# Routed tokens: from a placement table with gathered rows to a DRAM region per expert with dense tiles

## What is computed

```
logits = flat @ gate_W.T                       # 8 experts
probs = softmax(logits);  top_v, top_i = top_k(probs, 2)
g = silu(flat @ w1_e[e]);  u = flat @ w3_e[e]  # F = 512
out_e = (g * u) @ w2_e[e]
routed = sum over the two chosen experts of top_v * out_e
shared = the same form with shared weights, 512 wide in all, / 8
ffn = 0.5 * shared + 0.5 * routed
```

## Time and profile before

| | us |
|---|---|
| median of three timed runs | 782.5 (780.04 to 783.66) |
| the profiled execution, span from first to last instruction | 859.9 |
| TensorE busy | 717.7 (83%) |
| VectorE busy | 447.1 (52%) |
| ScalarE busy | 348.5 (41%) |
| GpSimd busy | 427.7 (50%) |

### The profile page before, as it was taken

How to read it: one execution, slowest core, us unless ns; L and a number is a source line. 1 busy time by engine, 2 the same in 40 slices (tenths; PEclk the granted TensorE clock), 3 DMA queues, 4 the chain that set the end, 5 groups by cost and what they waited for, 6 DMA issues and landing times.

```text
span 859.9 us, 12865 instructions
## 1 busy us (share of the span) xinstructions
PE 717.7 (83%) x4282; PEld 591.9 (69%) x4282; DVE 447.1 (52%) x1089; ACT 348.5 (41%) x913; POOL 427.7 (50%) x499
## 2 busy tenths in 40 slices
PE   3863998988888988985887687998998988888996
PEld 3742877877776767873565475786876777777874
DVE  7689743323233333425999977953333332323437
ACT  3622622323333233445775535831333332323433
POOL 6439052465555646347898524033365656555430
PEclk9985898999999999997999997998999999999999
DMA  9600010111111111021110010001111111111128
GB/s 317 230 1 0 1 37 17 30 43 37 40 38 37 42 34 44 25 85 58 40 39 24 26 50 0 2 25 25 28 41 35 43 34 43 37 40 36 31 71 247
DMA packets 45021, 43.75 MB, mean 51 GB/s; under 512 B 5984, under 2 KB 39776, under 8 KB 44576
## 3 DMA queue, kind: packets, MB, share of 16 engines
q1 hardware_dynamic: 35872, 24.32, 9.2%
q0 software_dynamic: 9088, 18.63, 7.8%
HBM read 27.33 MB, written 15.60 MB: 50 GB/s over the span
## 4 chain that ended last, share of the span: by engine, by line
issue 40%; PE 36%; DVE 8%; ACT 3%; another core or an unknown queue 2%; DMA 1%; SPq 0%; POOL 0%; DVEq 0%; ACTq 0%
PE psY L1463 8%; PE psH L1446 4%; PE psH L1375 3%; PE psG L1306 3%; PE psG L1304 2%; PE psG L1305 2%; PE psU L1306 2%; PE psU L1304 2%; PE psU L1305 2%; DVE rec L1045 1%; PE psG L1529 1%; PE psU L1562 1%; ACT silu L1190 1%; PE psT L1403 1%
## 5 line engine op out<-in xcount | busy, mean ns | idle before, releaser
L638 POOL DMA_INDIRECT results<-yout,target x142 | 139.7, 984 | 182.3 <-DVE yout L949 144.2
L745 DVE TENSOR_TENSOR hr<-silu,psU 128x512 f32<-128x512 f32 x142 | 97.3, 685 | 252.2 <-ACT silu L1190 129.4
L623 POOL DMA_INDIRECT rows<-tokens,source x142 | 137.0, 965 | 137.8 <-issue 69.0
L1463 PE MATMUL psY<-W,hT 128*128 x1120 | 152.6, 279 | 18.2 <-issue 12.2
L1190 ACT ACTIVATE silu<-psG 128x512 f32<-128x512 f32 x142 | 85.1, 599 | 203.6 <-PE psG L1306 148.7
L1463 PEld LDWEIGHTS psY<-W,hT 128*128 128x128 f32 x1120 | 135.9, 192 | 29.6 <-issue 22.9
L1183 ACT ACTIVATE hT<-psH 128x512 f32<-128x512 f32 x142 | 84.7, 596 | 110.5 <-remote 57.2
L1446 PE MATMUL psH<-ident,hr 128*128 128x128 f32 x568 | 86.4, 275 | 26.4 <-DVE hr L745 26.4
L1446 PEld LDWEIGHTS psH<-ident,hr 128*128 128x128 f32 x568 | 68.6, 141 | 53.2 <-DVE hr L745 37.8
L745 DVE TENSOR_TENSOR hs<-silu,psU 128x512 f32<-128x512 f32 x64 | 43.4, 683 | 59.0 <-PE psU L1306 30.8
L1375 PEld LDWEIGHTS psH<-W2S,hs 128*128 128x128 f32 x512 | 65.9, 210 | 8.1 <-DVE hs L745 6.9
(11 more groups left out here) (187 smaller groups left out, 1266.1 us busy)
## 6 DMA issues: line engine op xcount, KB each, us to landing
W<-w_e SPq DMA_DIRECT2D x3, 2048.0 KB, 13.4
tokens<-XN SPq DMA_DIRECT2D x16, 256.0 KB, 3.1
Y<-results SPq DMA_DIRECT2D x32, 128.0 KB, 2.3
YF<-results SPq DMA_DIRECT2D x16, 256.0 KB, 5.1
rows<-tokens,source POOLq DMA_INDIRECT x142
results<-yout,target POOLq DMA_INDIRECT x142
X<-x SPq DMA_DIRECT2D x8, 256.0 KB, 5.6
out<-X SPq DMA_DIRECT2D x8, 256.0 KB, 2.6
```

Of the source, the lines that this page charges most:

```text
L623: pool.indirect_dma_start(rows[:, g % RING, t, :], None, tokens, bass.IndirectOffsetOnAxis(ap=source[:, tile:tile + 1], axis=0))\
L638: pool.indirect_dma_start(results, bass.IndirectOffsetOnAxis(ap=target[:, tile:tile + 1], axis=0), yout[:, g % 2, t, :], None).then_inc(y_ ...
L745: dve.tensor_tensor(hidden, silu[:, s.u % 2, :], psU[:, s.u % 2, :], ALU.mult).then_inc(h_done, 1)
L1463: i = pe.matmul(into[:, t * D:(t + 1) * D], hT[:, s.u % 2, f, :], W2[:, bass.ds(at + f * D, D)], start=(f == 0), stop=(f == FT - 1))
```

## The change

A token row gets two more words, its own number and its second place (ROW = 130). DRAM holds a region of 4224 rows for each expert (`slots`). Routing is done in five batches of 4, 4, 8, 8 and 8 token tiles (`ROUTES`): for each, VectorE finds the top two and, after TensorE's count, the place of each pair in its expert's region, and GpSimd scatters each token tile twice, once for each chosen expert, with one indirect DMA each (`scatter`, 64 a layer). The tiles of an expert are then dense rows of its region, whose start VectorE works out once (`find_tiles`, 20 operations). SyncE writes 128 rows of zeros at the end of each expert's rows and fetches each tile with a plain DMA from an address that it loads from SBUF (`fetch_rows`). The targets of the results are found group by group from the two words that come with the rows (`aim_group`, four small operations on VectorE). The placement table, its batches on three engines, the tensor `tokens` and its eight writes a layer are gone. The low parts of the transposed tokens are made by VectorE and not by GpSimd; of the expert weights ScalarE makes the high parts and VectorE the low parts. GpSimd keeps the scale factors of the layer norm and sends the results, with no fetches between. The gate product has 8 columns and not 128. Steps are placed by the tables below, from a few steps before the first shared step. `FRONT` and the rest of the routed part stay as they were.

```diff
+ROUTES = [(0, 4), (4, 4), (8, 8), (16, 8), (24, 8)]
+WIDEST = max(n for _, n in ROUTES)
+ROW = D + 2
+REGION = NT + P
+SLOTS = E * REGION
...
+FIRST = [-5, -7]
+LN_AT = [{-5: 0, -4: 1, -3: 2, -1: 3, 2: 4, 5: 5, 8: 6, 12: 7, 14: 8}, {-6: 7, -3: 8}]
+TOP_AT = [{-2: 0, 1: 1, 7: 2, 13: 3, 20: 4}, {-7: 0, -2: 1, 2: 2, 7: 3, 13: 4}]
+PLACE_AT = [{0: 0, 3: 1, 9: 2, 15: 3, 22: 4}, {-4: 0, 1: 1, 4: 2, 9: 3, 15: 4}]
+LOW_AT = [{-1: 0, 1: 1, 4: 2, 8: 3, 11: 4, 16: 5, 19: 6, 25: 7}, {-5: 0, -1: 1, 0: 2, 2: 3, 6: 4, 10: 5, 14: 6, 18: 7}]
+LOW_W_AT = {5: 0, 7: 1, 9: 2, 10: 3, 13: 4, 16: 5, 17: 6, 20: 7}
+TABLES_AT = [24, 17]
+GATES_AT = [26, 19]
+TURN_AT = [{-4: 0, -3: 1, 0: 2, 5: 3, 8: 4, 12: 5, 15: 6, 18: 7}, {-5: 6, -3: 7}]
+SCORE_AT = [{-3: 0, -2: 1, 2: 2, 6: 3, 9: 4, 13: 5, 18: 6, 20: 7}, {-6: 5, -2: 6, 0: 7}]
+RANK_AT = [{-1: 0, 3: 1, 10: 2, 16: 3, 23: 4}, {-5: 0, 2: 1, 6: 2, 11: 3, 17: 4}]
+HIGH_AT = [SCORE_AT[0], {-6: 0, -5: 1, -3: 2, -2: 3, 2: 4, 6: 5, 10: 6, 14: 7}]
+HIGH_W_AT = {k - 2: j for k, j in LOW_W_AT.items()}
+EXP_AT = [25, 18]
...
+                def fetch_rows(g):
+                    if g >= RING:
+                        sp.wait_ge(aimed, GROUPS * l + g - RING + 1)
+                    for tile in range(g * GT, min((g + 1) * GT, RUN)):
+                        at = sp.value_load(from_row[0:1, tile:tile + 1], min_val=0, max_val=SLOTS - P)
+                        sp.dma_start(rows[:, g % RING, tile % GT, :], slots[bass.ds(at, P), :])\
+                          .then_inc(rows_in[g % RING], 16)
+                sp.wait_ge(ends_done, l + 1)
+                for e in range(E):
+                    end = sp.value_load(ends[0:1, e:e + 1], min_val=0, max_val=SLOTS - P)
+                    sp.dma_start(slots[bass.ds(end, P), :], zeros[:, :]).then_inc(padded, 16)
+                sp.wait_ge(padded, 16 * E * (l + 1))
+                sp.wait_ge(from_done, l + 1)
+                sp.wait_ge(scattered, 16 * TOPK * TILES * (l + 1))
+                sp.wait_ge(u_full, shared_at(l, (RING + 1) * FT - 1) + 1)
+                for g in range(GROUPS):
+                    fetch_rows(g)
...
+                def scatter(b, first, last):
+                    start, n = ROUTES[b]
+                    if first == 0:
+                        pool.wait_ge(xn_done, CHUNKS * l + (start + n) // CH)
+                        pool.wait_ge(placed, len(ROUTES) * l + b + 1)
+                    for tile in range(start + first, start + last):
+                        for k in range(TOPK):
+                            pool.indirect_dma_start(
+                                slots, bass.IndirectOffsetOnAxis(ap=place[:, tile, 2 * k:2 * k + 1], axis=0),
+                                XN[:, tile, :], None).then_inc(scattered, 16)
+                def scale_next(c):
+                    if l == 0 or c >= POOL_AHEAD:
                         scale_ln(l, Step.of(c, 2))
+                for c in range(3):
+                    scale_next(c)
                 if l == 0:
...
+                    low_shared()
+                scale_next(3)
+                if l == 1:
+                    for c in range(4, CHUNKS):
+                        scale_next(c)
+                    for b, (_, n) in enumerate(ROUTES):
+                        scatter(b, 0, n)
+                else:
+                    scatter(0, 0, 4)
+                    scale_next(4)
+                    scatter(1, 0, 2)
+                    scale_next(5)
+                    scatter(1, 2, 4)
+                    scatter(2, 0, 2)
+                    scale_next(6)
+                    scatter(2, 2, 4)
+                    scale_next(7)
+                    scatter(2, 4, 8)
+                    scatter(3, 0, 8)
+                    scatter(4, 0, 8)
...
+                    if t == 0:
+                        pool.wait_ge(aimed, GROUPS * l + g + 1)
...
+                for g in range(GROUPS):
+                    for t in range(min(GT, RUN - g * GT)):
+                        send_result(g, t)
...
+                def top_two(b):
...
+                    if b > 0:
+                        dve.wait_ge(ranked, len(ROUTES) * l + b)
+                    route.then(dve.tensor_reduce(counted[:, :], both, X_AXIS, ALU.add))
+                    dve.tensor_copy(chosen_rows[:, :], counted[:, :]).then_inc(picked, 1)
...
+                def place_in(b):
+                    start, n = ROUTES[b]
...
+                    from_ = region[:, :] if b == 0 else taken_to[:, b - 1, :]
+                    dve.wait_ge(ranked, len(ROUTES) * l + b + 1)
+                    route.then(dve.tensor_tensor(base[:, :], from_, psY[:, RANKS_AT:RANKS_AT + E], ALU.add))
+                    dve.tensor_tensor(taken_to[:, b, :], from_, psY[:, RANKS_AT + E:RANKS_AT + 2 * E], ALU.add)\
+                       .then_inc(ranks_read, 1)
+                    route.then(dve.tensor_tensor(both[:, :, 0], base[:, :], both[:, :, 0], ALU.add))
+                    route.then(dve.tensor_tensor_scan(sums, not_first[n][:, :, :].rearrange("p e i -> p (e i)"),
+                                                      chosen[:, 0:n * E], 0.0, ALU.mult, ALU.add))
+                    for k in range(TOPK):
+                        route.then(dve.tensor_tensor(picks, sums.rearrange("p (e i) -> p i e", e=E),
+                                                     onehot[k][:, at, :], ALU.mult))
+                        route.then(dve.tensor_reduce(posf[:, at, k], picks, X_AXIS, ALU.add))
+                    route.then(dve.tensor_copy(place[:, at, 0:3:2], posf[:, at, :]))
+                    dve.tensor_copy(XN[:, at, D:ROW].bitcast(i32), place[:, at, 1:3]).then_inc(placed, 1)
...
+                def aim_group(g):
+                    tiles = slice(g * GT, min((g + 1) * GT, RUN))
+                    n = tiles.stop - tiles.start
+                    dve.wait_ge(rows_in[g % RING], fetched(l, g))
+                    if g == 0:
+                        dve.wait_ge(tables_done, l + 1)
+                    aims.then(dve.tensor_tensor(aim[:, 0, 0:n], rows[:, g % RING, 0:n, D + 1].bitcast(i32), own[:, tiles],
+                                                ALU.is_equal))
+                    aims.then(dve.scalar_tensor_tensor(aim[:, 1, 0:n], aim[:, 0, 0:n], float(NT),
+                                                       rows[:, g % RING, 0:n, D].bitcast(i32), ALU.mult, ALU.add))
+                    aims.then(dve.tensor_tensor(aim[:, 2, 0:n], aim[:, 1, 0:n], valid[:, tiles], ALU.mult))
+                    dve.tensor_tensor(target[:, tiles], aim[:, 2, 0:n], dump[:, tiles], ALU.add).then_inc(aimed, 1)
...
+                for k in range(FIRST[l], SHARED):
                     if k == front[l] + 6 % FT:
                         copy_xT(Step.of(0, 2 * GT))
+                        aim_group(0)
+                    if k in PLACE_AT[l]:
+                        place_in(PLACE_AT[l][k])
                     if k == done[0]:
                         shared_steps(1)
-                    for _ in range(PLAN[l].get(k, 0)):
-                        batch(taken)
-                        taken += 1
-                    if k == TABLE_STEP[l]:
-                        table()
-                        experts()
+                    if k in TOP_AT[l]:
+                        top_two(TOP_AT[l][k])
+                    if k in LN_AT[l]:
+                        ln_step(LN_AT[l][k])
+                    if k in LOW_AT[l]:
+                        low_xnT(LOW_AT[l][k])
+                    if l == 0 and k in LOW_W_AT:
+                        low_experts(LOW_W_AT[k])
+                    if k == TABLES_AT[l]:
+                        find_tiles()
+                    if k == GATES_AT[l]:
+                        weigh()
...
+                def high_experts(j):
+                    w, cols = j % 2, slice(j // 2 * WCOLS, (j // 2 + 1) * WCOLS)
+                    act.wait_ge(experts_in, 48)
+                    act.activation(W13H[:, w, cols], W13[:, w, cols], ACT.Copy).then_inc(w_high, 1)
```

More of the change, by code:

```diff
@@ L317, in macaron @@
              ("ha", [P, 2, TB * P], fp32)],
-            [("rows", [P, RING, GT, D], fp32)],
+            [("rows", [P, RING, GT, ROW], fp32)],
             [("XNTL", [P, NT], fp32r), ("XNTH", [P, NT], fp32r)])
@@ new lines, in find_tiles @@
+                def find_tiles():
+                    cmp3 = [P, TILES_R, E]
+                    last = taken_to[:, len(ROUTES) - 1, :]
+                    dve.wait_ge(ranks_read, len(ROUTES) * (l + 1))
+                    dve.tensor_scalar(ends[:, :], last, 1.0, None, ALU.add).then_inc(ends_done, 1)
+                    route.then(dve.tensor_tensor(counted[:, :], last, region[:, :], ALU.subtract))
+                    route.then(dve.tensor_scalar(tile_bits[:, 0, :], counted[:, :], float(P - 1), None, ALU.add))
@@ L929, in copy_xT_later, with aim_later @@
                         copy_xT(s)
+                def aim_later(s):
+                    if s.i > 0 and s.u % GT == 0:
+                        aim_group(s.over(GT))
```

(60 more changed lines are left out.)

437 lines of the change are left out of this document (142 added, 295 removed).

## The result

| | before | after |
|---|---|---|
| timed runs, median us | 782.09 (4 runs, 780.04 to 783.66) | 817.35 (4 runs, 814.8 to 818.64) |
| ratio to before | | 1.0444 [1.0424, 1.0465] |
| profiled execution, us | | 818.64 |
| span, granted clock | | 816.9 us, 0.942 |

The forecast was 798, slower; the range ended at 814. The direction and the main mechanism held; the size did not: of a loss of 35 us some 16 were expected.

A forecast was written before the change was run, and what follows sets the result against it. Placement masks on VectorE bound layer 0's front, TensorE the routed stage. Timed: 782.5 - 5.1 (layer 0) + 20.4 (layer 1) = 797.8 us, taken as 798; likeliest 790 to 812, wider range 752 to 814.

The forecast's parts named there:

- first step: Stalls of 66.1 + 7.6 + 6.4 = 80.1 us explain the profile's extra 77.4 us and are absent from timed runs.
- Rival 1: Indirect DMAs cost less without the profiler: 768 at 1.0 us each, some 766 at 0.8; chance 0.20.
- rival 3: Scatters cost 1.5 us, by the wider row or by locking: total 823 us; chance 0.10.
- layer 0, from there to the last scatter's end: Layer 0's front: 48 scatters x 1.27 = 61 us plus three ln scale factors, 3.1 us.
- layer 0, tail to the first routed product: Layer 0, behind the last scatter: landings, four SyncE loads and issues, transposes and splitting, sum 11.4 us.
- layer 1, chain: Layer 1's front: 64 scatters on GpSimd's queue, 63 x 1.27 + 0.97 = 81 us.
- 588.0 - 508.0: Layer 1 before the change: first routed product without the stall at 588.0, last attention addition ending at 508.01.
- With 4 us of waiting for X and the first scores: 51.: Layer 0's front: VectorE needs 43 us from 3.9 to place routes 0 to 2, plus 4 us of waits.
- So GpSimd is never without work.: Layer 1's front: route 4, placed some 44 us after the first, meets a queue of 48 scatters (61 us).
- Four transposes and two splitting operations ... 2.0.: Last part of the wait behind the last scatter, before the first routed product: 0.6 + 2 x 0.69 = 2.0 us.
- The rule weighed against the change: 2-port VectorE operations lock GpSimd out: 20 scalings lengthen layer 0's chain by up to 7.4 us, sum 805.
- only for this reason the removed masks bring so little: Layer 0's front: VectorE's 96 us of work ends about 105, covered by scatters whose last comes at 115.

The follow-up runs named there:

- experiment 1: The kernel before, unchanged, profiled a second time: 780.09 us, span 778.1.
- 3: The changed kernel with each of the 16 scatters of the fifth batch issued twice in each layer, the second into an unread spare tensor: 856.71 us.
- 8: The changed kernel with only the first of the two scatters of each token tile in layer 1, 32 instead of 64: 794.25 us.
- 2: The changed kernel with the last output block of each shared front moved ahead of the first transposes: 813.91 us.
- 4: The changed kernel with 28 instead of 24 shared steps ahead of layer 1's routed stage: 816.83 us.
- 6: The changed kernel with layer 1's second and third token batch placed one and two steps earlier: 811.84 us.
- 7: The changed kernel with VectorE's 8 weight-split subtractions replaced by a one-input operation that writes zeros: 814.01 us.
- 5: The kernel before with only the expert-weight splits moved off GpSimd, to 8 casts on ScalarE and 8 subtractions on VectorE: 759.95 us.

## Why the prediction was right in direction and wrong in size

**Right.** Its first step, that the 77 us by which the profile was long do not belong to the timed runs, is shown by experiment 1. So is the mechanism: 64 scatters a layer, 1.26 us apart, set both first routed products (3 and 8). The price per scatter, taken from the nearest row of another kind of indirect DMA, was right to 0.01 us, with rows of 520 bytes. Rival 1 (cheaper) and rival 3 (1.5 us) fall with it. The routed stages came out as said.

**Wrong: what stands around the 64 x 1.27.** Sizes, from the prediction's terms:

| term | predicted | measured | more |
|---|---|---|---|
| layer 0, start of the third batch | 51 | 56.8 | 5.8 |
| layer 0, from there to the last scatter's end | 64 | 66.1 | 2.1 |
| layer 0, tail to the first routed product | 11.4 | 14.0 | 2.6 |
| layer 1, last addition to first scatter | 8.0 | 9.5 | 1.5 |
| layer 1, chain | 81 | 87.5 | 6.5 |
| layer 1, tail | 11.4 | 13.9 | 2.5 |

Together 21.0. The 56.8 is the latest of six profiles with the same code up to there; the others (2, 3, 4, 6 and 8) have 55.4 to 56.5, so about 1 us of the first row is the difference between executions. Against before, in this profile layer 0 lost 5.0 instead of gaining 5.1 and layer 1 lost 32.2 instead of 20.4 (before itself stands 1.3 better there than the 588.0 - 508.0 assumed); the stretch between and the end add 1.7. The steps that failed:

- "With 4 us of waiting for X and the first scores: 51." A sum of busy times with a guess for the waits. VectorE's waits up to 57 us in after are 4.5 us for shared products, 4.3 for a GpSimd constant, 2.9 for the first scores and 1.4 for X: 13.1, where 3.9 and 4 were counted. This is 5.2 of the 5.8 in this profile.
- "So GpSimd is never without work." It was asked of route 4 only, the last. Batches 1 and 2 came too late by 1.8 and 4.4 us more than the usual 0.30; placing them one and two steps earlier took 5.5 us off the total (6).
- "Four transposes and two splitting operations ... 2.0." What the transposes stand ahead of was not followed: an output block of 32 products was queued behind their wait, 5.4 to 5.6 us long instead of 3.8, since TensorE had stood for over 20 us (granted clock 0.62 in 120:140). SyncE's part came out lower: 5.3 us from the first issue (125.60) to the transposes (130.85), where 8.1 had been put down, though that first issue came 2.7 us behind the last scatter's end (122.91) and not 1.3 (the 2.7 hold the first address load too). In sum SyncE's part and the landings were 1.5 us less than put down, and TensorE's and VectorE's part, from the transposes to the first routed product, 6.1 us instead of 2.0.
- The rule weighed against the change was applied to the wrong operation: rows of scalings held a scatter by 0.16 us at most, while the prediction's own 1.2 us weight splits held five scatters of layer 0 by 0.47 to 1.17 us, 4.4 us in all (7).
- Not priced at all: the routing of each batch between VectorE's gatings. It is covered by the chain in the changed kernel, yet layer 1's front stays 8.8 us longer than before when the chain is halved (8). So rival 1's 768 with cheaper scatters would have been too low. Its 766 for 0.8 us a scatter does not follow from its own terms either: with layer 0 held at 113, layer 1's chain, 63 x 0.2 us shorter, would bring 768 down to 755.

What the change gives is real as well: moving the weight splits alone is worth 21.9 us (5). So the rest of the change costs 817.35 - 759.95 = 57.4 us against that variant, and the net is 35.5 against the 781.85 of that comparison. The sentence "only for this reason the removed masks bring so little" was right for layer 0, but the prediction never priced that part by itself, and so did not see that the version to keep is the one with the splits moved and nothing else.

Open: which operations of VectorE with one SBUF input hold a scatter (the 128x1024 one did, the reductions did not), what exactly makes layer 1's front 8.8 us longer without the chain, and why the first profile of before was 77 us long.

## What to carry to other kernels

Before you put work on one engine's queue that a whole stage waits for, count instructions times their start-to-start time; then check for every batch, not only the last, that its input is ready when the queue gets there. Follow the bounding wait on the engine that waits: what is queued behind it, and at which clock it will run. And where a change joins several edits, price and run them apart: here one gained 22 us and the rest lost 57.

## What was not expected of the hardware

- An indirect DMA of GpSimd that begins while VectorE runs an operation with two SBUF inputs is held until 0.12 to 0.14 us before that operation ends (73 of 73 cases, held by up to 1.05 us). One that begins within 0.03 us of it does not hold it, unless another was running before; one that begins 0.13 us or more later, or one that reads PSUM (164 cases), does so by 0.08 us at most.
- Four fetches by SyncE with addresses from a table: 5.3 us (layer 0) and 5.5 (layer 1: 572.18 to 577.65) from the first issue to the transposes that read them, landing (1.8 us) included.
- TensorE after 16 us of waiting runs its next ten products at 0.80 and 0.63 us instead of 0.48 and 0.40 (experiment 2); an output block, at 5.4 instead of 3.8, had borne this before.
- One profiled execution of the same program had a span of 859.9 us, the next 778.1. The profile's own time against the timed median is the first thing to read.
